# Two of eight low halves and half a sum moved between engines in the opening of a GRU and expert kernel

## The reference

```
def cell(h, x):
    gi = x @ W_ih + b_ih
    gh = h @ W_hh + b_hh
    i_r, i_z, i_n = jnp.split(gi, 3, axis=-1)
    h_r, h_z, h_n = jnp.split(gh, 3, axis=-1)
    r = jax.nn.sigmoid(i_r + h_r)
    z = jax.nn.sigmoid(i_z + h_z)
    n = jnp.tanh(i_n + r * h_n)
    h_new = (1.0 - z) * n + z * h
    return (h_new, h_new)
...
scores = jnp.einsum('btd,ed->bte', x, Wg)
topk_s, topk_i = jax.lax.top_k(scores, TOP_K)
probs = jax.nn.softmax(topk_s, axis=-1)
...
for e in range(E):
    h = jax.nn.silu(jnp.einsum('btd,hd->bth', x, W1[e])) * jnp.einsum('btd,hd->bth', x, W2[e])
    y = y + w[..., e:e + 1] * jnp.einsum('bth,dh->btd', h, W3[e])
```

## Time and profile before

| | us |
|---|---|
| median of 3 runs | 1429.38 |
| lowest, highest | 1427.17, 1432.07 |
| the profiled execution, its own time | 1434.45 |
| its span, first to last instruction | 1432.7 |
| first matmul of step 0 | 39.73 |

### The profile page before, as it was taken

How to read it: one execution, slowest core, us unless ns; L and a number is a source line. 1 busy time by engine, 2 the same in 40 slices (tenths; PEclk the granted TensorE clock), 3 DMA queues, 4 the chain that set the end, 5 groups by cost and what they waited for, 6 DMA issues and landing times.

```text
span 1432.7 us, 79346 instructions
## 1 busy us (share of the span) xinstructions
PE 1337.3 (93%) x33080; PEld 1151.4 (80%) x33080; DVE 1054.0 (74%) x4216; ACT 760.0 (53%) x2166; POOL 398.8 (28%) x847
## 2 busy tenths in 40 slices
PE   2888888899999999999999999999999999988997
PEld 1787777888888888988888988888888888864564
DVE  7688888877777777777777777777777777764342
ACT  6677776554555554555454555554545555543443
POOL 1001112223232322223333222322223332235443
PEclk9899998999999999999999999999999999999999
DMA  8445523334434443444433333444344444355752
GB/s 283 131 136 143 135 69 106 78 66 72 72 68 75 81 77 78 73 74 75 81 62 78 72 68 76 81 77 77 70 72 81 69 71 72 60 91 97 112 92 36
DMA packets 248032, 124.90 MB, mean 87 GB/s; under 512 B 190463, under 2 KB 223231, under 8 KB 247680
## 3 DMA queue, kind: packets, MB, share of 16 engines
q1 hardware_dynamic: 229728, 86.17, 29.2%
q0 software_dynamic: 17952, 33.64, 13.4%
HBM read 59.12 MB, written 35.72 MB: 66 GB/s over the span
## 4 chain that ended last, share of the span: by engine, by line
PE 74%; DVE 12%; DMA 8%; issue 4%; ACT 1%; POOL 1%; SPq 0%; DVEq 0%; POOLq 0%; ACTq 0%
PE gi_ps L1479 15%; PE gn_bank L1456 12%; PE gz_ps L1456 12%; PE b_ps L1510 7%; PE y_ps L1526 7%; PE gr_ps L1447 6%; PE a_ps L1510 6%; PE gr_ps L1441 6%; DMA out_y<-wih,mt 4%; DMA out_y<-work,mt 3%; DVE wexp L1122 2%; PE b_ps L1479 1%; DVE hn L1152 1%; DVE hn L1158 1%; DVE gi L1104 1%
## 5 line engine op out<-in xcount | busy, mean ns | idle before, releaser
L1479 PE MATMUL gi_ps<-xs,wih 128*128 128x128 f16 (+1 forms) x4464 | 248.2, 214 | 3.9 <-issue 3.0
L1456 PE MATMUL gn_bank<-hlog,whh 128*128 128x32 f16 x8192 | 245.8, 177 | 4.3 <-issue 4.3
L1456 PE MATMUL gz_ps<-hlog,whh 128*128 128x32 f16 x8192 | 245.9, 177 | 3.2 <-issue 3.0
L719 POOL DMA_INDIRECT out_y<-work,mt x57 | 93.4, 1638 | 513.5 <-PE gz_ps L1456 491.9
L1479 PEld LDWEIGHTS gi_ps<-xs,wih 128*128 128x128 f16 x4464 | 229.3, 98 | 7.5 <-issue 4.8
L1456 PEld LDWEIGHTS gn_bank<-hlog,whh 128*128 128x128 f16 x8192 | 224.4, 96 | 5.0 <-issue 5.0
L906 ACT ACTIVATE rpre<-rpre,sc 128x64 f32<-128x64 f32 x256 | 88.5, 346 | 263.1 <-DVE rpre L1139 260.0
L1456 PEld LDWEIGHTS gz_ps<-hlog,whh 128*128 128x128 f16 x8192 | 224.5, 96 | 4.0 <-issue 4.0
L1441 PEld LDWEIGHTS gr_ps<-hlog,whh 128*128 128x128 f16 x4096 | 131.0, 96 | 61.3 <-DVE hlog L1167 37.5
L1441 PE MATMUL gr_ps<-hlog,whh 128*128 128x16 f16 x4096 | 141.1, 170 | 32.8 <-DVE hlog L1167 31.6
L1447 PE MATMUL gr_ps<-hlog,whh 128*128 128x32 f16 x4096 | 142.0, 176 | 1.4 <-issue 1.4
(11 more groups left out here) (214 smaller groups left out, 2286.8 us busy)
## 6 DMA issues: line engine op xcount, KB each, us to landing
wexp<-in_w_units SPq DMA_DIRECT2D x46, 256.0 KB, 4.0
x_raw<-in_x_feat SPq DMA_DIRECT2D x32, 256.0 KB, 3.5
h_tok<-xrow SPq DMA_DIRECT2D x32, 256.0 KB, 3.1
out_y<-in_x_tok SPq DMA_DIRECT2D x24, 192.0 KB
out_y<-in_x_tok SPq DMA_DIRECT2D x28, 128.0 KB
wexp<-in_w_hh SPq DMA_DIRECT2D x4, 768.0 KB, 7.3
wexp<-in_w_inproj SPq DMA_DIRECT2D x4, 768.0 KB, 12.4
wexp<-in_w_units SPq DMA_DIRECT2D x15, 192.0 KB, 4.0
```

Source lines behind the costliest of these rows:

```text
L719: pool.indirect_dma_start(out=out, out_offset=bass.IndirectOffsetOnAxis(ap=mt[:, j % RING, 0:1].bitcast(I32), axis=0), in_=ysc[y_slot(j)], ...
L1456: mm = pe.matmul(dst[:, j], whh[:, i, k, m * P:(m + 1) * P], h[:, k], start=False, stop=True, skip_group_check=True)
L1479: mm = pe.matmul(BATCH_BANKS[bank][:, (m - first) * width:(m - first + 1) * width], wih[:, p, w_part, (b * K + k) * P:(b * K + k + 1) * P] ...
```

## The change

Six edits, all about the opening:

- DVE no longer makes the low half of W_hh piece 0. GpSimd does, with a new helper `spare_low`: a `tensor_scalar` that writes the scaled piece in fp32 to a scratch in slot 6 of `wexp`, and a `tensor_tensor` that subtracts the high half. It waits for the high half (`whh_hi` 1). PE waits for it ahead of step 0.
- DVE no longer makes the low half of W_ih piece 3. GpSimd does it in the same way, behind `wi_scaled`, the high half and its own first piece. PE's projection of piece 3 waits for `pool_low` 2 instead of DVE's fourth.
- ACT makes the high half of piece 3 first, ahead of 1 and 2, and so DVE's `wi_low(p)` waits for p + 1 high halves instead of p.
- Of the last W_hh magnitude sum ACT takes 768 of the 1536 columns, and DVE a `tensor_reduce` over the other 768.
- SP issues only five of the nine groups of raw expert weights in the opening: those of expert 0 and the first two of expert 1. The third of expert 1 goes to step 0, expert 2's to steps 1 to 5.
- SP at step 1 and ACT ahead of expert 2's high halves wait for `pool_low` 2, since the scratch lies where expert 2's weights come.

```
+    FIRST_RAW = {0: ((1, 2, 0, None),), 1: ((2, 0, 0, 2),), 2: ((2, 0, 2, None),), 3: ((2, 1, 0, 2),),
+                 4: ((2, 1, 2, None),), 5: ((2, 2, 0, None),)}
...
+        prep_scaled = place(6, 0, MW * K * P)
...
             def load_raw(t):
+                if t == 1:
+                    sp.wait_ge(pool_low, 2)
+                for e, w, lo, hi in FIRST_RAW.get(t, ()):
+                    load_units(e, w, lo, hi)
...
-            for e in range(3):
-                for w in range(3):
-                    load_units(e, w)
+            for e, w in ((0, 0), (0, 1), (0, 2), (1, 0), (1, 1)):
+                load_units(e, w)
...
+            def spare_low(out, raw, high, s):
+                G.tensor_scalar(scaled[:, 0:raw.shape[1]], raw, s, None, ALU.mult).then_inc(pool_scaled, 1)
+                n_scaled[0] += 1
+                pool.wait_ge(pool_scaled, n_scaled[0])
+                return G.tensor_tensor(out, scaled[:, 0:raw.shape[1]], high, ALU.subtract)
...
+            pool.wait_ge(whh_hi, 1)
+            spare_low(whh[:, 1, 0], whh_raw[:, 0], whh[:, 0, 0], scale(SC_W)).then_inc(pool_low, 1)
+            pool.wait_ge(wi_scaled, 1)
+            pool.wait_ge(wi_hi, 1)
+            pool.wait_ge(pool_low, 1)
+            spare_low(wih[:, WI - 1, 1], wi_raw(WI - 1), wih[:, WI - 1, 0], wi_sc[:]).then_inc(pool_low, 1)
...
-                                act.wait_ge(wi_lo, WI)
+                                act.wait_ge(wi_lo, WI - 1)
+                                act.wait_ge(pool_low, 2)
...
-                S.activation(prep_junk, whh_raw[:, k], ACT.Abs, accum_out=mags[:, k:k + 1]).then_inc(whh_mag, 1)
+                half = M * P if k < K - 1 else M * P // 2
+                S.activation(prep_junk[:, 0:half], whh_raw[:, k, 0:half], ACT.Abs, accum_out=mags[:, k:k + 1]
+                             ).then_inc(whh_mag, 1)
...
-            for p in range(1, WI - 1):
+            for p in (WI - 1, *range(1, WI - 1)):
                 wi_high(p)
             measure(0, 0)
-            wi_high(WI - 1)
...
-                    dve.wait_ge(wi_hi, p)
+                    dve.wait_ge(wi_hi, p + 1)
...
+            dve.wait_ge(whh_loaded[K - 1], 16)
+            chain(V.tensor_reduce(mags[:, 4:5], whh_raw[:, K - 1, M * P // 2:M * P], AX_X, ALU.add,
+                                  apply_absolute_value=True))
...
-            for k in (*range(ACT_HIGHS, K), *range(ACT_HIGHS)):
+            for k in (*range(ACT_HIGHS, K), *range(1, ACT_HIGHS)):
...
-            for p in range(WI):
+            for p in range(WI - 1):
                 wi_low(p)
...
-                        pe.wait_ge(wi_lo, p + 1)
+                        if p < WI - 1:
+                            pe.wait_ge(wi_lo, p + 1)
+                        else:
+                            pe.wait_ge(pool_low, 2)
...
+            pe.wait_ge(pool_low, 1)
             for t in range(T):
                 recur(t)
```

More of the change, by code:

```diff
@@ L320, in y_slot @@
             return 0 if j < MAIN_TILES else (j + 1 - MAIN_TILES) % 3
+        scaled = prep_scaled
         asum = sb("asum", [P, 2])
@@ L406, in gru_moe_kernel @@
         consts = sem("consts")
+        pool_scaled = sem("pool_scaled")
+        pool_low = sem("pool_low")
         setup = sem("setup")
@@ L688, in _ @@
             G = nc.gpsimd
-            n_list = [0]
+            n_list, n_scaled = [0], [0]
             def chain(ins):
@@ L1359, in _ @@
             chain(V.tensor_tensor(wg[:, :, :, 1], wg_scaled[:], wg[:, :, :, 0], ALU.subtract))
+            dve.wait_ge(whh_loaded[K - 1], 16)
+            chain(V.tensor_reduce(mags[:, 4:5], whh_raw[:, K - 1, M * P // 2:M * P], AX_X, ALU.add,
+                                  apply_absolute_value=True))
             dve.wait_ge(whh_mag, K)
-            chain(V.tensor_reduce(mags[:, 4:5], mags[:, 0:4], AX_X, ALU.add))
-            exponents(prep_bits[:, 0:1], prep_exp[:, 0:1], mags[:, 4:5]).then_inc(prep_measured, 1)
+            chain(V.tensor_reduce(mags[:, 7:8], mags[:, 0:5], AX_X, ALU.add))
+            exponents(prep_bits[:, 0:1], prep_exp[:, 0:1], mags[:, 7:8]).then_inc(prep_measured, 1)
             dve.wait_ge(prep_turned, 1)
```

## The result

| | before | changed |
|---|---|---|
| median us (13 runs each) | 1429.38 | 1436.80 |
| lowest, highest | 1426.14, 1432.69 | 1432.49, 1439.53 |
| span of the profiled execution | 1432.7 | 1437.8 |
| `whh_scaled` | 17.71 | 16.48 |
| `wi_scaled` | 29.68 | 32.22 |

The ratio is 1.0052 (95% interval 1.0042 to 1.0062), 7.4 us slower; the forecast was 1435.4, 6.0 slower. Beside three other kernels on a second chip, where the kernel before had 1436.31, the changed one came to 1.0029 (1.0013 to 1.0044). The two intervals share only 1.0042 to 1.0044, some 6 us; the estimates by themselves are 7.4 and 4.2 us. One run of the changed kernel there took 1972 us and one of the kernel with half the sum alone 2182, where all others lie within 1% of their medians; both are left out of the figures.

The account below looks back on a forecast made before the run. The opening was taken to end at DVE, ACT close behind. Opening +7.25, PE's clock +0.8 and loads -2.0 made +6.0 us: 1440.5 for the profiled execution, 1435.4 for the median, range 1424.5 to 1440.

Parts of the forecast that it names:

- That each excludes the other, and GpSimd gets its turn: Opening: GpSimd's reading instructions and DVE's low halves take turns, opening +7.25 us; 1435.4 us in all, chance 0.5.
- Rival 1: Opening: GpSimd works beside DVE without exclusion, step 0 at 36.7, 1424.9 us in all; chance 0.3.
- rival 2: Opening: exclusion, but DVE keeps its turn, W_hh low halves end at 24.9; 1431.4 us in all; chance 0.2.
- The price of the pair: GpSimd's two instructions for one low half: 1.7 plus 3.6, 5.3 us, between 3.2 and 10.7.
- the sign asked for: Profile after: GpSimd's two-input instruction of 1536 columns far longer than twice its one-input one, as one sign of being right.
- W_hh: W_hh low halves: DVE's three and GpSimd's pair in one row where four of DVE's stood, +3.55 us.
- W_ih: From `wi_scaled` to step 0: GpSimd alternates with DVE's low halves, PE has pieces 2 and 3 left, +4.35 us.
- The clock term: Projection pieces 2 and 3: PE's clock may fall after idling, 1.7 us more for 72 matmuls, half taken, +0.8.
- The shared sum: Last W_hh magnitude split between ACT and DVE: -0.65 us up to `whh_scaled`.
- The loads: Moved expert loads: the 1.96 us stall in step 0 should go, -2.0 us, between 0 and -3.
- The rest of the way: From step 0 on steps hang on each other, so the opening's gain or loss reaches the launch's end one to one.

Follow-up runs that it names:

- the probes: Two kernels: the kernel before plus GpSimd instructions with unused results, in the second also DVE ones beside them; run once each, 1434.12 and 1432.58 us.
- TensorE busy: The changed kernel with 12 and 11 extra unused matmuls of 512 columns ahead of projection pieces 1 and 2; ratio 1.0047 to the kernel before.

## Why the prediction was right

- **That each excludes the other, and GpSimd gets its turn**: right. DVE's held rows are 4.5 to 4.7 us long in all five profiles that have the edit, and the probes show with what: GpSimd's reads against a second SBUF input. The rule of the Trainium skill (SBUF — State Buffer, Who interferes with whom) is borne out in whom it names, a two-input instruction held (2.25 us for 0.6), a one-input reduce not (0.95). It is not borne out in that the pair is taken for the whole instruction: the next point has a DVE row that needs 1.82 us and ends 0.72 behind GpSimd's. Rival 1 would have needed rows of 1.82 us beside GpSimd's, rival 2 a W_hh run that ends at 24.9; it ended at 29.89.
- **The price of the pair**: 5.3 us was near what DVE lost, for a wrong reason, and that is luck. The one-input instruction took 4.0 once DVE's is out of the way (1.7 forecast, 3.5 the upper bound; 2.22 for half the columns alone). The two-input one has rows of 3.59 and 3.61 (3.6 forecast), but each begins 0.64 or 0.65 us before the held low half of DVE ends; less that it is 2.95, an estimate that fits the 1.64 of half the columns, as 3.6, more than twice that, would not. So the sign asked for, a two-input row far longer than twice the one-input one, did not come. A MEMSET's row is no measure for an instruction that reads. But DVE's two held low halves stretched by only 2.92 + 2.71 = 5.63 us in the first pair and 2.80 + 2.82 = 5.62 in the second, not by the 7.0 of the two instructions: DVE's row ends just 0.72 us behind the end of `tensor_scalar` and 1.61 behind that of `tensor_tensor`, with 1.82 of its own to do each time. The exclusion seems to end about 1.1 and 0.2 us ahead of the ends of these rows, which makes up the difference; why, was not tried.
- **W_hh**: +3.55 forecast; `whh_scaled` to `wi_scaled` went from 11.97 to 15.74, +3.77.
- **W_ih**: +4.35 and +0.8 for the clock; `wi_scaled` to step 0 went from 10.05 to 16.30, +6.25. DVE took 12.35 instead of 11.9 (and 8.2 before, until 37.89, not 8.1 as the sum has it). The clock term should have been taken whole: 72 matmuls in 4.00 us, against 2.27 with TensorE busy, are 1.7.
- **The shared sum**: -0.65 forecast. `whh_scaled` came 1.23 earlier. ACT's row for the last piece began at 13.38 instead of 14.00, so 0.62 of that is W_hh landing sooner; from there to `whh_scaled` it was 3.10 instead of 3.71, and this 0.61 is the edit. At the end nothing of it can be measured.
- **The loads**: -2.0. Step 0 to step 1 became 3.3 us shorter than in the first profile, stall and half clock together. By the traces the term was attached to the wrong part: the kernel with GpSimd's low halves alone has no stall either, and its step 0 is 3.4 us shorter. With step 0 late, the transfers are over before it, and the moved loads have nothing left to save there; in the kernels with an early step 0 they are worth 4 us. The medians can neither confirm nor deny that: +9.0 for GpSimd alone and -4.1 for the loads alone would be +4.9, and the change measured 7.4 and 4.2. The term was also taken against one profile: its stall of 1.96 us was 0.59 in the second profile of the same kernel.
- **The rest of the way**: the forecast held the early steps' gain and loss to reach the end one to one. Single profiles don't: the second profile of the unchanged kernel falls behind the first by 6.6 us from step 16 to 48, where idle stretches of PE of the kind counted above and half-clock stretches lie differently, and the changed one by 2.0. The medians decide, not the spans.

## What to carry to other kernels

Before an elementwise piece goes from VectorE to GpSimd, look at what VectorE runs meanwhile: beside instructions with two SBUF inputs GpSimd's reads add most of their time to VectorE's (5.6 us for the two of a pair, to save a low half of 1.85), beside a one-input reduce they cost nothing, and memsets cost the two-input instructions nothing. The trace of before held the sign, in tiny GpSimd rows that ended with a long VectorE row. Of several edits made together one can hide another's gain: with the low halves back on VectorE, the moved loads and the shared sum came out 0.12% and 0.35% faster than before in two measurements, the loads alone 0.28% and 0.29%.

## What had not been expected

GpSimd's one-input `tensor_scalar` with a pointer scalar on fp32 is slower than its two-input `tensor_tensor`: 2.22 against 1.64 us on 768 columns, and on 1536, less the time in which VectorE held them, 4.0 against some 2.95. Its memset of 1536 fp32 columns took 1.4 us. And a TensorE kept busy through two gaps held its clock at 2.4 GHz and won 1.7 us in the opening that no median showed.
